# Rebuilding the start of a gated cross-attention kernel: keys by batch on GpSimd, the first queries in token halves on VectorE

## The reference

```python
q = _rms_norm(_layernorm(x), q_norm_w)
k = _rms_norm(ctx, k_norm_w)          # v = ctx
...
q = q * cos + _rotate_half(q) * sin
k = k * cos + _rotate_half(k) * sin
scores = jnp.einsum('bgnqd,bgkd->bgnqk', qg, k) * scale
attn = jax.nn.softmax(jnp.where(causal, scores, -1e+30), axis=-1)
x = x + jnp.tanh(g_xattn[0]) * (out @ w_out.T)
x = x + jnp.tanh(g_ffn[0]) * ffn(_layernorm(x), ...)
```

## Time and profile before

| | us |
|---|---|
| median of 3 runs | 474.4 |
| the three runs | 471.44, 474.4, 1056.45 |
| profiled execution | 474.46 |
| its span (first to last instruction) | 472.7 |

### The profile page before, as it was taken

One profiled execution on the slowest core, in us unless ns is written; L12 is line 12 of the kernel. 1 busy time (PEld: TensorE's weight loads), 2 busy tenths in 40 slices (PEclk: granted clock), 3 DMA queues, 4 the chain that ended last, 5 costly groups with the idle time before them and its releaser, 6 DMA issues.

```text
span 472.7 us, 10263 instructions
## 1 busy us (share of the span) xinstructions
PE 414.6 (88%) x3135; PEld 360.4 (76%) x3150; DVE 383.1 (81%) x1185; ACT 273.8 (58%) x617; POOL 286.1 (61%) x385
## 2 busy tenths in 40 slices
PE   0179997979898899999999999999999996678994
PEld 0067885767686799899899899898998985667894
DVE  5885769686779988798897788888888868767997
ACT  2026654545333766857677676677677678175440
POOL 5947627902289667677587587687677544163551
PEclk9999999989999999999999999999999998799998
DMA  8200000200235695685675865855955664000011
GB/s 282 55 1 3 2 1 3 85 5 3 46 67 110 140 199 118 155 189 113 163 155 110 200 144 110 190 128 112 224 120 109 148 81 96 11 0 2 0 46 44
DMA packets 71347, 44.53 MB, mean 94 GB/s; under 512 B 57360, under 2 KB 59536, under 8 KB 71312
## 3 DMA queue, kind: packets, MB, share of 16 engines
q1 hardware_dynamic: 67392, 35.42, 35.5%
q10 hardware_dynamic: 3920, 8.69, 6.1%
HBM read 13.68 MB, written 1.05 MB: 31 GB/s over the span
## 4 chain that ended last, share of the span: by engine, by line
PE 62%; DVE 20%; POOL 7%; issue 5%; DMA 3%; ACT 2%; SPq 0%; ACTq 0%; POOLq 0%; DVEq 0%
PE bank L1272 34%; PE bank L1387 5%; PE bank L1340 5%; DVE yacc L1127 3%; PE bank L1339 2%; PE bank L1388 2%; DVE yacc L1136 2%; POOL room L435 2%; PE bank L1212 2%; PE bank L1253 2%; DVE nxm L902 2%; PE bank L1190 2%; DMA rows_sb<-in_rows 1%; PE bank L1169 1%; PE bank L1213 1%
## 5 line engine op out<-in xcount | busy, mean ns | idle before, releaser
L631 ACT ACTIVATE probs<-turned 128x768 uint16<-128x768 uint16 x64 | 69.0, 1079 | 20.8 <-DMA turned<-halves 19.4
L639 ACT ACTIVATE probs<-sm,nm 128x128 f32<-128x128 f32 (+1 forms) x128 | 56.9, 445 | 40.9 <-DVE nm L1013 40.6
L1272 PE MATMUL bank<-hH,qk_parts 128*128 128x512 f32 x240 | 75.4, 395 | 0.0
L447 POOL COPY halves<-probs 128x768 uint16<-128x768 uint16 x64 | 52.8, 824 | 33.7 <-DVE probs L1059 33.7
L435 POOL TENSOR_TENSOR room<-room,qk_room 128x512 f32<-128x512 f32 x32 | 41.3, 1293 | 34.5 <-DMA qk_room<-qk_room 29.5
L1272 PE MATMUL bank<-hL,qk_parts 128*128 128x512 f32 x120 | 57.7, 481 | 0.9 <-DVE room L930 0.9
L1272 PEld LDWEIGHTS bank<-hH,qk_parts 128*128 128x128 f32 x240 | 45.2, 188 | 9.5
L930 DVE SCALAR_TENSOR_TENSOR room<-bank,qk_bias,cst_sb 128x512 f32<-128x512 f32 x64 | 47.4, 741 | 0.0
L1272 PE MATMUL bank<-woH,o_parts 128*128 128x256 f32 x256 | 47.3, 283 | 0.0
L1272 PE MATMUL bank<-woL,o_parts 128*128 128x256 f32 x128 | 38.8, 303 | 8.3 <-DVE o_parts L1001 2.7
L435 POOL TENSOR_TENSOR room<-room,q_room 128x512 f32<-128x512 f32 x32 | 41.2, 1288 | 5.6 <-DMA q_room<-q_room 5.5
(11 more groups left out here) (216 smaller groups left out, 1267.8 us busy)
## 6 DMA issues: line engine op xcount, KB each, us to landing
qk_room<-qk_room SPq DMA_DIRECT2D x64, 128.0 KB, 2.4
q_room<-q_room SPq DMA_DIRECT2D x64, 128.0 KB, 2.4
stg<-in_wqkv ACTq DMA_DIRECT2D x6, 768.0 KB, 5.5
stge<-in_we ACTq DMA_DIRECT2D x7, 256.0 KB, 3.1
stg<-in_wqkv SPq DMA_DIRECT2D x2, 768.0 KB, 6.3
stgo<-in_wo ACTq DMA_DIRECT2D x6, 256.0 KB, 3.4
x_sb<-in_x SPq DMA_DIRECT2D x4, 256.0 KB, 6.1
turned<-halves SPq DMA_TRANSPOSE x64, 2.9
```

Of the source, the lines that this page charges most:

```text
L447: pool.tensor_copy(halves[:, j % 2, :, :], PR[:, j % 2, 0:384].bitcast(U16).rearrange("p (n h) -> p h n", h=2)).then_inc(s["b_split"], 1)
L631: act.activation(PTs[:, 1 - q, 0:384].bitcast(U16).rearrange("p (n h) -> p h n", h=2), turned[:, (j - 3) % 4, :, :].rearrange("p (h c) n - ...
L639: ins = act.activation(PR[:, q, a:e], sm[:, q, a:e], ACT.Exp, bias=nm[:, q, t:t + 1], scale=-1.0, accum_out=rs[:, q, t:t + 1])
L1272: ins = pe.matmul(outp, l, r, start=(m == 0), stop=(m == n - 1))
```

## The change

- Loads: SyncE sends the first piece of `x`, then only the part of the constants with the mask and the cross-attention's tables, and the identity apart; the other pieces of `x` wait until `x` 0 and the first rows have landed. ScalarE first asks for the 320 weights of the rows that the tables need, then for the context of batch 0; the rest of both comes later.
- Keys: a new function `keys(b)` on GpSimd makes one batch's keys in instructions 128 wide. `keys(0)` stands between the query tables of the two halves, `keys(1)`, `keys(2)` and `keys(3)` between calls of `prep`. The root (`k_scale`) is now applied after the rotation.
- First queries: `prep(0, 0)` is gone from GpSimd. VectorE rotates and splits the first half of heads itself, first for token tile 0, then, after `k_out(0)`, for tile 1.
- Slots: those of batch 0 are filled by ScalarE (`q_slots`, `k_slots`), which also makes the bfloat16 identity and mask.
- The turned queries of tile 1 go to another bank (`first_q`) and are copied by VectorE.
- VectorE's roots of the later tiles move into pieces 0 to 6, `norm_q(1)` behind the maxima of p = 2, `pack(1, 0)` to p = 8. `qn` gets two buffers, so that `norm_q` waits for `prep` of two batches back.
- `k_turn(1)` runs at k = 10 of batch 0, `k_turn(2)` and `k_turn(3)` at k = 7 of batches 1 and 2, each `k_out` at the next k.
- TensorE runs 28 products 512 wide whose results nobody reads, from when the identity is there.

The core of the diff:

```diff
+        def second_q_at(b, k):
+
+            return k - (4 if b == 0 else 3)
+
+        def next_k_at(b, k):
+
+            return b + 1 < B and k == (10 if b == 0 else 7)
...
                 sp.dma_start(x_sb[:, 2 * b:2 * b + 2, :], x_v[:, 2 * b:2 * b + 2, :]).then_inc(s[f"d_x{b}"], 16)
                 if b == 0:
-                    sp.dma_start(cst_sb[:, 0:C_RCOSQ], cst[:, 0:C_RCOSQ]).then_inc(s["d_cst"], 16)
+                    sp.dma_start(cst_sb[:, C_MASK + P:C_RCOSQ], cst[:, C_MASK + P:C_RCOSQ]).then_inc(s["d_cst"], 16)
+                    sp.dma_start(cst_sb[:, C_ID:C_ID + P], cst[:, C_ID:C_ID + P]).then_inc(s["d_ident"], 16)
+                    sp.wait_ge(s["d_x0"], 16)
+                    sp.wait_ge(s["d_rows"], 16)
             sp.dma_start(cols_sb[:, :], cols).then_inc(s["d_cols"], 16)
...
+            def keys(b):
+
+                both = lambda room: room.rearrange("p (t n) -> p t n", t=2)
+                kv = ctx_sb[:, 2 * b:2 * b + 2, :]
+                heads = lambda room: room.rearrange("p (n d) -> p n d", d=XD)
+                sines = WKS[:, :, :].rearrange("p t (g d) -> p (t g) d", d=XD)
+                kc = kv.rearrange("p t (g d) -> p (t g) d", d=XD)
+                pool.tensor_tensor(both(kf), kv, WKC[:, :, :], ALU.mult)
+                pool.tensor_tensor(heads(kf2)[:, :, 0:8], kc[:, :, 8:16], sines[:, :, 0:8], ALU.mult)
+                link(pool.tensor_tensor(heads(kf2)[:, :, 8:16], kc[:, :, 0:8], sines[:, :, 8:16], ALU.mult))
+                link(pool.tensor_tensor(kf, kf, kf2, ALU.add))
+                pool.wait_ge(s["k_scale"], 1 if b == 0 else 2)
+                link(pool.tensor_tensor(both(kr), both(kf), small[:, k_scale(b):k_scale(b) + 2].unsqueeze(2).to_broadcast([P, 2, 64]), ALU.mult))
+                part = kpack[:, 8 * b:8 * (b + 1), :, :]
+                for m in range(3):
+                    ins = pool.tensor_copy(part[:, :, m, :], heads(kr))
+                    if b == 0:
+                        ins.then_inc(s["k0_part"], 1)
+                        pool.wait_ge(s["k0_part"], m + 1)
+                    else:
+                        link(ins)
+                    if m < 2:
+                        link(pool.tensor_tensor(heads(kr), heads(kr), part[:, :, m, :], ALU.subtract))
+                if b == 0:
+                    return
+                pool.tensor_copy(part[:, :, 3:6, :], part[:, :, 0:3, :])
+                pool.tensor_copy(part[:, :, 6:8, :], part[:, :, 0:2, :]).then_inc(s["kpack_ready"], 1)
+                pool.wait_ge(s["kpack_ready"], b)
+
+            q_tables(0)
+            pool.wait_ge(s["wtab_ready"], 6)
+            pool.wait_ge(s["d_ctx"], 16)
+            keys(0)
+            q_tables(1)
...
-            prep(0, 0)
             prep(0, 1)
...
             prep(1, 0)
+            keys(1)
             prep(1, 1)
+            keys(2)
             prep(2, 0)
             prep(2, 1)
+            keys(3)
             prep(3, 0)
             prep(3, 1)
...
-            act.dma_start(ctx_sb[:, :, :], ctx_v).then_inc(s["d_ctx"], 16)
-            act.dma_start(rows_sb[:, :], rows.to_broadcast([P, R_END])).then_inc(s["d_rows"], 16)
+            act.dma_start(rows_sb[:, 0:R_BO], rows[:, 0:R_BO].to_broadcast([P, R_BO])).then_inc(s["d_rows"], 16)
+            act.dma_start(ctx_sb[:, 0:2, :], ctx_v[:, 0:2, :]).then_inc(s["d_ctx"], 16)
...
-            act.activation(small[:, 96:98], rows_sb[:, R_GX:R_GX + 2], ACT.Tanh).then_inc(s["tanh_done"], 1)
+            act.dma_start(ctx_sb[:, 2:NT, :], ctx_v[:, 2:NT, :]).then_inc(s["d_ctx"], 16)
+            act.dma_start(rows_sb[:, R_BO:R_END], rows[:, R_BO:R_END].to_broadcast([P, R_END - R_BO])).then_inc(s["d_rows"], 16)
...
+            def q_slots(X, t):
+
+                t0, t1 = (0, 2) if t is None else (t, t + 1)
+                v = qpack[:, X, t0:t1, :, :, :].rearrange("p t h s d -> p (t h) s d")
+                for m, (a, e) in enumerate(((1, 3), (4, 6), (7, 8))):
+                    if X == 0:
+                        act.wait_ge(s["q0_part"], 3 * t + m + 1)
+                    ins = act.activation(v[:, :, a:e, :], v[:, :, 3 * m:3 * m + 1, :].to_broadcast([P, 8 * (t1 - t0), e - a, XD]), ACT.Copy)
+                ins.then_inc(s["q0_ready"], 1)
...
+            q_slots(0, 0)
+            k_slots(0)
+            k_slots(1)
+            k_slots(2)
             q_evac(0, 0, 0)
-            q_evac(0, 0, 1)
+            q_slots(0, 1)
+            act.wait_ge(s["d_ctx"], 32)
+            for t in range(2, NT):
+                square(t)
...
             def norm_q(b):
-                if b:
-                    dve.wait_ge(s["q_parts"], 2 * b)
+                if b >= 2:
+                    dve.wait_ge(s["q_parts"], 2 * (b - 1))
                 for t in range(2):
...
             norm_q(0)
-            link(dve.tensor_tensor(kr, ctx_sb[:, :, :], SM(34, 8).unsqueeze(2).to_broadcast([P, NT, 64]), ALU.mult))
...
+            dve.wait_ge(s["qn_ready"], 1)
+            for t in range(2):
+                if t == 1:
+                    k_out(0)
+                dve.wait_ge(s["q_table"], t + 1)
+                cut = slice(t * P, (t + 1) * P)
+                f, g, r = (v[:, cut].rearrange("p (h d) -> p h d", d=XD) for v in (first_qf, first_qf2, first_qr))
+                q = qn[:, 0, t, 0:P].rearrange("p (h d) -> p h d", d=XD)
+                w = WS[:, 0, t, :].rearrange("p (h d) -> p h d", d=XD)
+                dve.tensor_tensor(first_qf[:, cut], qn[:, 0, t, 0:P], WC[:, 0, t, :], ALU.mult)
+                dve.tensor_tensor(g[:, :, 0:8], q[:, :, 8:16], w[:, :, 0:8], ALU.mult)
+                link(dve.tensor_tensor(g[:, :, 8:16], q[:, :, 0:8], w[:, :, 8:16], ALU.mult))
+                link(dve.tensor_tensor(first_qf[:, cut], first_qf[:, cut], first_qf2[:, cut], ALU.add))
+                part = qpack[:, 0, t, :, :, :]
+                for m in range(3):
+                    dve.tensor_copy(part[:, :, 3 * m, :], r if m else f).then_inc(s["q0_part"], 1)
+                    dve.wait_ge(s["q0_part"], 3 * t + m + 1)
+                    if m < 2:
+                        link(dve.tensor_tensor(r, r if m else f, part[:, :, 3 * m, :], ALU.subtract))
+            dve.memset(small[:, 110:111], 0.0).then_inc(s["q_parts"], 1)
...
-            k_out(0)
-            pack(0, 0)
-            stats(2, NT)
-            k_out(1)
-            link(dve.tensor_scalar(SM(48, 6), mv[:, 2:NT, 1], 1.0 + EPS, EPS * EPS, ALU.mult, ALU.add))
-            rsqrt_seed(SM(48, 6), SM(56, 6), SM(124, 6))
-            rsqrt_step(SM(124, 6), SM(56, 6), SM(130, 6), 6)
-            k_out(2)
-            rsqrt_step(SM(124, 6), SM(56, 6), SM(130, 6), 6)
-            k_out(3)
-
+            dve.wait_ge(s["q_first_pe"], 1)
+            dve.tensor_copy(qT[:, 0, 1, :, :].rearrange("p h n -> p (h n)"), first_q[:, :]).then_inc(s["q_first"], 1)
...
                 if p < NPX:
                     x_max(p)
                 if p == 0:
-                    rsqrt_step(SM(124, 6), SM(56, 6), SM(130, 6), 6)
+                    stats(2, 4)
                 if p == 1:
-                    pack(0, 1)
-                if k == 1 and b + 1 < B:
+                    link(dve.tensor_scalar(SM(42, 2), mv[:, 2:4, 1], 1.0 + EPS, EPS * EPS, ALU.mult, ALU.add))
+                    rsqrt_seed(SM(42, 2), SM(54, 2), SM(70, 2))
+                    rsqrt_step(SM(70, 2), SM(54, 2), SM(82, 2), 2)
+                if p == 2:
+                    rsqrt_step(SM(70, 2), SM(54, 2), SM(82, 2), 2)
+                    rsqrt_step(SM(70, 2), SM(54, 2), SM(82, 2), 2)
+                if p == 3:
+                    stats(4, NT)
+                if p == 4:
+                    dve.wait_ge(s["ssk_done"], NT)
+                    dve.tensor_scalar(SM(48, 6), SM(10, 6), XD / 64, XD * EPS, ALU.mult, ALU.add)
+                    link(dve.tensor_scalar(SM(44, 4), mv[:, 4:NT, 1], 1.0 + EPS, EPS * EPS, ALU.mult, ALU.add))
+                    rsqrt_seed(SM(44, 10), SM(56, 10), SM(72, 10))
+                if p in (4, 5, 6):
+                    rsqrt_step(SM(72, 10), SM(56, 10), SM(84, 10), 10)
+                if p == 6:
+                    dve.memset(small[:, 110:111], 0.0).then_inc(s["k_scale"], 1)
+                if k == (2 if b == 0 else 1) and b + 1 < B:
                     norm_q(b + 1)
+                if k and next_k_at(b, k - 1):
+                    k_out(b + 1)
...
-                if k == 6 and b + 1 < B:
+                if k == (8 if b == 0 else 6) and b + 1 < B:
                     pack(b + 1, 0)
                 if k == 11 and b + 1 < B:
                     pack(b + 1, 1)
...
+            for _ in range(28):
+                pe.matmul(bank[6][:, :].rearrange("p (a n) -> p a n", a=4), ident_bf, ident_bf.unsqueeze(1).to_broadcast([P, 4, P]), start=True, stop=True)
+            q_turn(0, 0, 0)
             k_turn(0)
-            q_turn(0, 0, 0)
-            k_turn(1)
             q_turn(0, 0, 1)
-            k_turn(2)
-            k_turn(3)
```

(6 more changed lines are left out.)

143 lines of the change are left out of this document (80 added, 63 removed).

## The result

| | before | after |
|---|---|---|
| median, us | 474.56 (20 runs) | 476.22 (20 runs) |
| lowest, us | 471.44 | 473.78 |
| profiled span, us | 472.7 | 474.1 |

The ratio of after to before is 1.0036, with a 95% interval from 1.0020 to 1.0051; one of the twenty runs before took 1056.45 us, and the ratio goes by the fast runs. By the bound of 2% this is no change; with 20 runs on each side it is a small loss of 1.7 us. The prediction was 471.0 with a range from 464.5 to 475.5, so the time lies above the range, on the other side of the kernel before.

What follows compares the result with a forecast made beforehand. The prediction took a serial preparation at the start, with a full loop behind it, as the bound. It summed 474.46 - 5.1 + 0.8 + 0.5 + 0.3 = 470.96, so 471.0 us, range 464.5 to 475.5.

Steps and rivals of the forecast that it cites:

- new wait: VectorE waits for GpSimd in front of `pack(1, 1)`: takes 5.2 of 10.3 us gained at the first maxima.
- first maxima to batch 1's queries: On VectorE: three maxima 2.1, statistics 1.06, roots 1.6 and `norm_q` 0.7 sum to 5.5 us, queries ready at 26.0.
- GpSimd's chain: From `norm_q(1)` to the end of `prep(1, 1)`: 11.2 us for both `prep` plus 5.1 for `keys(1)`, ending at 42.3.
- Landing and tables: At the start: rows land at 4.7, `x` at about 4.6, saving 0 to 2.4 us; `keys(0)` ends at 12.4.
- Idle products: TensorE's 28 products start near 6.0 and last 7.7 us, a quarter at slow clock, until 13.7.
- Rival 2: Start on TensorE: idle products too long, ending at 18.0, or rows late; no or almost no gain, 475.0; chance 0.2.
- Contention: GpSimd and VectorE slowing each other: at most 9 us on GpSimd's 16.3 us chain, taken as 0.5.
- Rival 3: `norm_q(1)` to `prep(1, 1)`: contention stretches GpSimd's work to 27.5 us, p = 12 at 54.2, 481.5 us; chance 0.07.
- The margin: Kernel before, at `pack(1, 1)`: GpSimd's parts were ready 2.1 us earlier, so batch 1's preparation is just hidden.
- Rival 1: At `pack(1, 1)`: no wait, the whole 10.3 us lead survives, 465.0 us; chance 0.15.
- 0.8 for moved turns: `k_turn` and `k_out` of batches 2 and 3, moved into the loop, cost 0 to 2.6 us, taken as 0.8.
- The clock: TensorE's clock may drop after the wait ahead of `pack(1, 1)`: 0 to 1.8 us, taken as 0.3.

Runs made afterwards that it cites:

- e3: Changed kernel with 20 idle products on TensorE instead of 28; 474.74 us, ratio to before 1.0003.
- e4: Changed kernel with GpSimd beginning `prep(0, 1)` only when VectorE is done with token tile 1 of the first queries; 473.38 us, ratio to before 0.9968.
- e6: Changed kernel with 20 idle products, `prep(0, 1)` held behind tile 1, and batch 1's statistics, roots and `norm_q(1)` moved into VectorE's pauses before the loop; 472.67 us.
- e1: Changed kernel with `keys(1)` ahead of `prep(1, 0)` on GpSimd and key roots made earlier by VectorE; 477.61 us, ratio to before 1.0055.
- e2: Changed kernel with `pack(1, 1)` at p = 14 instead of p = 11; 477.19 us, ratio to before 1.0058.
- e7: Changed kernel with 20 idle products and batch 1's statistics, roots and `norm_q(1)` ahead of the loop, `prep(0, 1)` not held back; 473.95 us, ratio 0.9988.
- first pair of traces: Original profiles of the kernels before and after; the second pair traced both again without edit, one execution each at 471.92 and 476.95 us.

## Why the prediction was wrong

The prediction summed -5.1 at p = 12 and +1.6 of smaller terms; the profiled spans gave +0.5 at p = 12 and +0.9 behind it. The failed step is the first of these: "Of 10.3 us gained at the first maxima 5.2 go to a new wait of VectorE in front of `pack(1, 1)`, and 5.1 stay." Of 6.9 us gained at the first maxima 6.0 went to longer pieces 0 to 5 and 2.2 to the step into p = 12, with the new wait (0.96) in it; pieces 6 to 10 gave 0.8 back, and nothing stayed. The wait was there and ended by GpSimd's last cast, as forecast, but VectorE itself reached `pack(1, 1)` only at 46.38.

By its own terms, p = 12 was put at 43.0 and came at 48.58:

| term | predicted | measured | off |
|---|---|---|---|
| tile 1 can begin on VectorE | 15.5 | 17.29 | +1.8 |
| tile 1's work | 2.5 | 4.36 | +1.9 |
| tile 1's end to the first maxima | 2.5 | 2.26 | -0.2 |
| first maxima to batch 1's queries | 5.5 | 6.1 | +0.6 |
| GpSimd's chain | 16.3 | 17.2 | +0.9 |
| `pack(1, 1)` | 0.7 | 1.24 | +0.5 |

- **Landing and tables.** `x` was used at 5.01 instead of 4.6, and the tables began at 5.68 instead of 4.7, with the constants, not the rows, landing last. So `keys(0)` ended at 13.42 instead of 12.4, and ScalarE's slots of the keys were ready at 14.84 instead of 13.7. In after the idle products lasted beyond that and hid it; without them most of the delay would have come from here, as in e3, where the keys' transposes wait for these slots and begin at 15.08 instead of 15.97.
- **Idle products.** They began at 6.58 instead of 6.0 and took 8.94 until the first transpose instead of 7.7. Rival 2 had this mechanism with a chance of 0.2 and the sign by which to know it, transposes straight behind the last product; the other half of its sign, an end behind 17, did not come. It cost up to 1.7 us at the first transposes, and less behind the keys' slots, as e3 shows, not 4.
- **Contention.** With the start of tile 1 (+1.8, made of the two causes above) this was the largest term of the sum that was mis-sized. Rival 3 put it on GpSimd's chain and priced the sum with 0.5 there, "because in the loop VectorE mostly reads PSUM". The chain did take only 0.9 more, a wait included. But VectorE's own tile 1, for which the prediction took the undisturbed 2.4 us, stood beside `prep(0, 1)`, and e4 gives its price: 1.6 to 2.1 us there. The prediction had cited the rule for exactly these instructions and then charged GpSimd alone for it. Its reading of the rows was short there: the slot copies of `pack(1, 0)`, which took 1.65 us instead of 0.68 beside `prep`, stood in the same trace. And its bound, "at most 9 on the 16.3 us chain", does not agree with the 27.5 of its own rival 3, which is 11.2 above 16.3; neither was reached.
- **The margin.** That "the preparation of batch 1 is just hidden, by 2.1 us" holds for `pack(1, 1)` alone. In front of `pack(1, 0)` VectorE already waited 1.20 us for GpSimd (the row at 39.62). The change moved that copy two pieces on, and the wait is gone.
- **What lies behind the wait.** "Without this wait they would come 17.3 us behind the first, at 37.8" is wrong, and with a first maximum on time it would have been wrong too. The prediction counted the moved statistics and roots as a delay of `norm_q(1)` and not as work between the maxima. Pieces 0 to 5 took 6.0 us longer; e6 shows it for pieces 0 to 2, for pieces 3 to 5 it is read from the rows (VectorE busy for 6.53 of 6.87) and was not tested. e1 and e2 tell what lay behind: without the wait p = 12 comes 24.2 or 23.3 us behind the first maxima, not 17.3. In e7, without the wait and with pieces 0 to 2 relieved, it is still 21.6: against before, +4.0 in pieces 3 to 5 (7.12 for 3.16), +1.3 in the step to p = 12 with `k_out(1)` and the slowed copies, -1.1 in pieces 0 to 2. Rival 1, the whole lead, was for that reason not open at all.
- **Work behind p = 12.** Of the +1.6 only the 0.8 for moved turns lies there. From p = 12 to p = 36 the changed kernel took 0.7 us longer in the first pair of traces and 0.4 in the second (`pack(2, 0)` waits 0.66, and `k_out(2)` stands whole at 61.06 with 0.68). So this term was about right. That the whole +1.6 is near the +0.9 of the spans is luck: behind p = 36 the spans hold -0.9 for a lower clock in the kernel before and +1.1 between T2 and T14, which nobody had in the sum.
- **The clock.** The expected loss behind `pack(1, 1)` did not come (1.00 in the row from 36.83 on). It came at the second transposes, which took 0.4 us more for it on the path to the first maxima, and in the pieces 0 to 2 (0.54), where VectorE bounds anyway.
- **The range.** Its upper end of 475.5 lay 0.7 us under the median. Products and contention stood in rivals, each alone and the contention on the other engine; the moved work as time between the maxima stood in none. All three came true together.

What is shown: contention on tile 1 (e4), that the first three pieces are filled by the moved work (e6), and that of a lead of 6.9 and 8.2 us at the first maxima hardly any is left at p = 12 (0.5 behind in one pair of traces, 0.7 ahead in the other). What is only in part: the 1.7 us by which the end is above before. 0.35 us of it lies outside the spans: a run before took 1.75 to 1.88 us more than its span, every run of the changed kernel 2.08 or more, 2.17 in the median, and no run here shows why. At T0 the changed kernel stands 0.3 behind in the first pair and 1.2 in the second; with the stretch from p = 36 to 47 taken at its short length in all four, 1.2 behind and 0.3 ahead. A further 0.8 to 1.1 us, at a clock of 1.00, lies from T2 to T14, in code that the change did not touch, and its cause stays open.

## What to carry to other kernels

When a start is made shorter by moving work behind it, count that work twice: as a delay of what waits for it and as time of the engine in the loop that it enters. Before a wait is priced, write down where the next limit lies, because taking the wait away gains only the distance to that. And where a trace shows two engines slowing each other, charge both of them, at the place where each is on the critical path.

## What the hardware did that I had not expected

- VectorE's nine instructions on 128x128 and 128x64 took 2.39 us alone and 4.36 beside GpSimd's `prep`; a product with two SBUF operands 64 wide went from 0.22 to 0.75, and a cast with one operand from 0.23 to 0.65.
- The same 28 idle products took from 7.67 to 8.94 us until the transposes behind them, by when their distance fell from 0.43 to 0.22 us (at 9.8 or at 12.4), and they kept their effect only until the next pause: transposes at 15.52 took 0.61 for eight, and after 5.4 us without work, with a granted clock of 0.50, 1.04.
- One and the same kernel, with the granted clock at 0.93 or 1.00 for a stretch of self-attention, took 48.61 or 46.36 us for it. The fall came in 2 us in which TensorE was busy for 0.42, but 2 us of the same kind in the other execution brought none. A median over few runs of this kernel therefore moves by a microsecond or two without any edit.
